# Two routing-weight matmuls folded into one, and short contractions padded to 128 rows, in a four-stage transformer kernel

## The reference

```python
x = x + tanh(g_xattn[0]) * L0_xattn(layernorm(x), ctx)
x = x + tanh(g_ffn[0])   * L0_ffn(layernorm(x))      # the mixture of experts
x = x + tanh(g_xattn[1]) * L1_xattn(layernorm(x), ctx, mask)
x = x + tanh(g_ffn[1])   * L1_ffn(layernorm(x))      # weights looked up in a table of 16
```

```python
# L0_ffn: 16 experts of width 64, the best 4 per token, and a shared expert of width 64
probs = softmax(h @ gate_w.T);  w, chosen = top_k(probs, 4);  w = w / w.sum()
comb[token, expert] = w where chosen, else 0
out = sum_e comb[:, e] * ((silu(h @ Wg[e]) * (h @ Wu[e])) @ Wd[e])
    + sigmoid(h @ shared_gate_w) * ((silu(h @ sWg) * (h @ sWu)) @ sWd)
# L1_ffn: width 688 = 5 * 128 + 48
out = (silu(h @ G.T) * (h @ U.T)) @ Dn.T
```

## Time and profile before

| | |
|---|---|
| median of three runs | 521.7 us |
| the profiled execution | 521.62 us, of which 519.8 us is the span from the first to the last instruction |
| TensorE | busy 436.0 us, 84% of the span |
| VectorE | 352.4 us, 68% |
| ScalarE | 199.7 us, 38% |
| GpSimd | 173.2 us, 33% |
| mean granted TensorE clock | 0.890 |

### The profile page before, as it was taken

One profiled execution on the slowest core, in us unless ns is written; L12 is line 12 of the kernel. 1 busy time (PEld: TensorE's weight loads), 2 busy tenths in 40 slices (PEclk: granted clock), 3 DMA queues, 4 the chain that ended last, 5 costly groups with the idle time before them and its releaser, 6 DMA issues.

```text
span 519.8 us, 9005 instructions
## 1 busy us (share of the span) xinstructions
PE 436.0 (84%) x3024; PEld 400.1 (77%) x3024; DVE 352.4 (68%) x769; ACT 199.7 (38%) x391; POOL 173.2 (33%) x207
## 2 busy tenths in 40 slices
PE   0465866958477999999998999989999998989996
PEld 0444856847367999999998988968987897788885
DVE  5767577584505668585855887798698879756642
ACT  2346445355220434343332443444354253423331
POOL 3104133231400221212134533653564355333332
PEclk9958785959657999999998969989987998999999
DMA  8111010100200020200101001001001000000000
GB/s 248 29 61 62 0 61 0 32 31 0 101 1 0 1 102 0 78 23 27 74 0 54 1 6 48 0 0 52 0 0 51 1 0 0 0 2 20 20 20 21
DMA packets 6629, 15.96 MB, mean 31 GB/s; under 512 B 1091, under 2 KB 4292, under 8 KB 6101
## 3 DMA queue, kind: packets, MB, share of 16 engines
q1 hardware_dynamic: 6612, 15.75, 9.2%
HBM read 14.70 MB, written 1.05 MB: 30 GB/s over the span
## 4 chain that ended last, share of the span: by engine, by line
PE 33%; issue 31%; POOL 15%; DVE 11%; ACT 6%; DMA 2%; POOLq 1%; DVEq 0%; ACTq 0%; SPq 0%
PE ps L289 19%; PE ps L484 5%; POOL workr L1010 4%; DVE work L1292 4%; PE ps L1086 3%; POOL work L1344 3%; POOL workr L1468 2%; PE ps L474 2%; POOL workA L565 2%; ACT workA L509 1%; POOL wB_lo L571 1%; POOL rstd L254 1%; PE ps L1098 1%; PE ps L359 1%; POOL wB_lo L1349 1%
## 5 line engine op out<-in xcount | busy, mean ns | idle before, releaser
L289 PE MATMUL ps<-xT_hi,wB_hi 128*128 128x256 f32 x224 | 65.7, 293 | 1.7 <-POOL wB_lo L1349 1.7
L289 PE MATMUL ps<-xT_lo,wB_hi 128*128 128x256 f32 x224 | 64.1, 286 | 0.0
L289 PE MATMUL ps<-xT_hi,wB_lo 128*128 128x256 f32 x224 | 63.9, 285 | 0.0
L289 PE MATMUL ps<-wB_hi,workr 128*128 128x256 f32 (+1 forms) x224 | 52.1, 296 | 4.5 <-POOL workr L1468 3.4
L289 PE MATMUL ps<-wN_hi,shared_r 128*128 128x256 f32 x256 | 52.8, 302 | 0.0
L1344 POOL TENSOR_SCALAR work<-work,lut_step,lut 128x344 f32<-128x344 int32 (+1 forms) x72 | 46.3, 659 | 1.7 <-POOL wB_lo L1349 1.6
L1010 POOL TENSOR_TENSOR workr<-work,workr 128x256 fp32r<-128x256 f32 (+1 forms) x36 | 22.9, 637 | 71.7 <-ACT workr L893 71.7
L1292 DVE COPY_PREDICATED work<-work 128x1376 f32<-128x1376 int32 (+5 forms) x36 | 43.6, 1212 | 4.0 <-DVE work L1292 1.1
L289 PEld LDWEIGHTS ps<-xT_hi,wB_hi 128*128 128x128 f32 x224 | 43.4, 194 | 2.4 <-issue 1.9
L289 PEld LDWEIGHTS ps<-wN_hi,shared_r 128*128 128x128 f32 x256 | 44.0, 206 | 1.5 <-DVE shared_r L1255 1.5
L289 PEld LDWEIGHTS ps<-wB_hi,workr 128*128 128x128 f32 (+1 forms) x224 | 38.4, 189 | 7.5 <-issue 6.2
(11 more groups left out here) (183 smaller groups left out, 1128.8 us busy)
## 6 DMA issues: line engine op xcount, KB each, us to landing
stage<-in_wC SPq DMA_DIRECT2D x4, 1280.0 KB, 5.5
stage<-in_wB SPq DMA_DIRECT2D x4, 768.0 KB, 4.3
stage<-in_idx SPq DMA_DIRECT2D x4, 536.0 KB, 4.0
stage<-in_wA SPq DMA_DIRECT2D x2, 512.0 KB, 5.4
out<-x SPq DMA_DIRECT2D x4, 256.0 KB, 2.2
x<-in_x SPq DMA_DIRECT2D x1, 768.0 KB, 6.7
ctx_T<-in_ctx_T SPq DMA_DIRECT2D x1, 512.0 KB, 7.1
ctx_n<-in_ctx_n SPq DMA_DIRECT2D x4, 128.0 KB, 2.1
```

The lines of the kernel that those rows point to most:

```text
L289: last = nc.tensor.matmul(out, l, r, start=start and i == 0, stop=stop and i == 2)
```

## The change

The two halves of the transposed routing weights go into one tile, `comb_rows`: the upper weights in rows 0 to 16, the lower ones in rows 32 to 48. `sel` has its table twice, in rows 0 to 16 and in rows 32 to 48. One matmul over 128 rows then gives the sum of both. In setup, one memset of GpSimd goes and ScalarE copies `sel` twice; the SyncE wait counts one more. The down products of the shared expert (before 64 rows) and of the last step of stage D (before 48 rows) run over all 128 rows. The added rows meet zeros: `sd` is padded with zero rows, and the padded gate columns of stage D are zero. In stage D the elementwise work of that step is now over 128 rows too; in stage B it stays at 64.

```diff
@@ constants, wS
+LOWER = 32
-            return (..., w[0:F, n:n + D],
+            return (..., w[:, n:n + D],
@@ act_A_start
-            act.wait_ge(padded, 3)
-            nc.scalar.copy(sel[0:E + 1]..., stage[0:E + 1, 0:NSEL]).then_inc(setup_act, 1)
+            act.wait_ge(padded, 2)
+            for r in (0, LOWER):
+                nc.scalar.copy(sel[r:r + E + 1]..., stage[0:E + 1, 0:NSEL]
+                               ).then_inc(setup_act, 1)
@@ tiles of stage B
-        combT_hi, combT_lo = (take_r(TG) for _ in range(2))
+        comb_rows = take_r(TG)
+        combT_hi, combT_lo = comb_rows[0:E + 1], comb_rows[LOWER:LOWER + E + 1]
@@ pe_B: spread(k)
-                nc.tensor.matmul(o, sel[:, k, :], combT_hi, start=True, stop=False)
-                nc.tensor.matmul(o, sel[:, k, :], combT_lo, start=False, stop=True).then_inc(*Bp["bc_done"].up())
+                nc.tensor.matmul(o, sel[:, k, :], comb_rows, start=True, stop=True).then_inc(*Bp["bc_done"].up())
@@ pe_B: down(k)
-                n = rows_B(k)
-                    last = mm3(ps[:, 6 + t, 0:D], h_hi[k % 3][0:n, t * P:(t + 1) * P],
-                               h_lo[k % 3][0:n, t * P:(t + 1) * P], d_hi, d_lo, k == 0, k == EC)
+                    last = mm3(ps[:, 6 + t, 0:D], h_hi[k % 3][:, t * P:(t + 1) * P],
+                               h_lo[k % 3][:, t * P:(t + 1) * P], d_hi, d_lo, k == 0, k == EC)
@@ stage D
         def rows_D(k):
-            return P if k < FC - 1 else FLAST
+            return P
@@ sync and tensor, setup
-            sp.wait_ge(setup_act, 2)
+            sp.wait_ge(setup_act, 3)
@@ gpsimd, setup
-            nc.gpsimd.memset(combT_hi.bitcast(F32), 0.0).then_inc(padded, 1)
-            nc.gpsimd.memset(combT_lo.bitcast(F32), 0.0).then_inc(padded, 1)
+            nc.gpsimd.memset(comb_rows.bitcast(F32), 0.0).then_inc(padded, 1)
```

More of the change, by code:

```diff
@@ L178, in wS @@
             n = DC * 2 * F
-            return (w[:, 0:n].rearrange("p (c n) -> p c n", c=DC), w[0:F, n:n + D],
+            return (w[:, 0:n].rearrange("p (c n) -> p c n", c=DC), w[:, n:n + D],
                     w[:, n + D:].rearrange("p (c n) -> p c n", c=DC))
@@ L630, in act_A_start @@
             act.wait_ge(sel_in, 16)
-            act.wait_ge(padded, 3)
-            nc.scalar.copy(sel[0:E + 1].rearrange("p k n -> p (k n)"), stage[0:E + 1, 0:NSEL]).then_inc(setup_act, 1)
+            act.wait_ge(padded, 2)
+            for r in (0, LOWER):
+                nc.scalar.copy(sel[r:r + E + 1].rearrange("p k n -> p (k n)"), stage[0:E + 1, 0:NSEL]
+                               ).then_inc(setup_act, 1)
         def act_A(act, g, more, two_more):
@@ L907, in act_B @@
             act.wait_ge(*Bp["combT_done"].at(g, 1))
-            nc.scalar.copy(combT_hi[0:E + 1], combT).then_inc(*Bp["combT_hi"].up())
+            nc.scalar.copy(combT_hi, combT).then_inc(*Bp["combT_hi"].up())
             upper(0)
@@ L983, in dve_B @@
             dve.wait_ge(*Bp["combT_hi"].at(g, 1))
-            nc.vector.tensor_tensor(combT_lo[0:E + 1], combT, combT_hi[0:E + 1].bitcast(F32),
+            nc.vector.tensor_tensor(combT_lo, combT, combT_hi.bitcast(F32),
                                     ALU.subtract).then_inc(*Bp["combT_lo"].up())
@@ L1522, in _ @@
             pe.wait_ge(setup_dve, 6)
-            pe.wait_ge(setup_act, 2)
+            pe.wait_ge(setup_act, 3)
             pe.wait_ge(*A["x_done"].at(GROUPS, 0))
```

## The result

| | Kernel before | Changed kernel |
|---|---|---|
| first comparison: median (lowest to highest of 14 runs) | 521.84 us (520.67 to 524.01) | 518.14 us (516.96 to 523.73) |
| ratio, 95% interval | | 0.994 (0.991 to 0.996) |
| a later comparison: median | 522.55 us (17 runs) | 520.14 us (12 runs) |
| ratio, 95% interval | | 0.995 (0.992 to 0.998) |
| profiled execution: time, span, clock | 521.62, 519.8 us, 0.890 | 521.0, 519.2 us, 0.887 |

The forecast was 517.6 us and faster; it came out at 518.1 and faster. The profiled execution of the changed kernel lay in the upper half of its runs. So the two spans must not be subtracted; what can be compared are periods of the same stretch at the same clock.

A forecast was written before the change was run, and what follows sets the result against it. TensorE was taken as the bound, with three waits per stage B group. Spread matmuls 3.84 plus D's row changes 0.27 gave 4.11 us off 521.62: 517.5, or 517.6 on the median; range 516.2 to 519.1.

The forecast's parts named there:

- The three points where TensorE waits: Stage B group: TensorE waits ahead of spread(0) 0.26 us, down(6) 0.35 and down(8) 0.31; gapless between.
- point 2: Stage B, ahead of down(6): TensorE waits 0.35 us for GpSimd's lower part, a chain starting at the end of gate_up(8).
- The spread matmuls: Stage B: 36 go at 0.12 us; spread(0) to spread(6) gain 0.84, spread(7) 0, spread(8) 0.12; 3.84 us over four groups.
- point 1: Stage B, ahead of spread(0): TensorE waits 0.26 us for VectorE's lower routing weights, timed by the end of the group before.
- 128 rows: Row change at group boundaries: 0.09 us each, 0.27 over three in D, 0 in B; entry free, added elementwise work 0.
- B's exits: Stage B, leaving the short product at group boundaries: gain 0, as VectorE is later at spread(0); other bound 0.27 us.
- Setup, 0: ScalarE's second sel copy, 1.15 us, taken as hidden in idle times: 0, bounded by 0 and 1.15.
- Halfway: Rival: slack at down(1) or VectorE mid-group runs out, half of 3.84 turns into waits; 519.7 us, chance 0.08.
- setup: Rival: the sel copy stands in the chain of waits and all of 1.15 us stays; 518.7 us, chance 0.05.
- nothing: Rival: the removed matmul was hidden, so the change does nothing; 521.6 us, chance 0.02.
- The rival with the row change at entries and B's exits: Rival: row change also costs at entry, 0.09 in 8 places, 0.72 us more, or B's exits count; 516.8 us, chance 0.04.
- The slower one: Rival: less dense TensorE work brings half-clock stretches in stage B, 1.5 us per group; 523.4 us, chance 0.03.

The follow-up runs named there:

- more3: Changed kernel with three further copies of spread(3)'s matmul in each group of B; groups of B 27.25, 27.24, 27.23 us.
- more7: Changed kernel with three further copies of spread(7)'s matmul in each group of B; groups of B 26.91, 26.88, 26.90 us.
- shift_only: Kernel before with two spread matmuls kept, but lower routing weights written to rows 32 to 48 and sel copied twice; ratio 1.0037 against the kernel before.
- aligned: Changed kernel with routing weights written twice side by side, so VectorE reads and writes rows 32 to 48 in place; ratio 0.9961 against the kernel before.
- twocopy: Changed kernel with halves exchanged: lower weights at rows 0 to 16, upper copied by ScalarE to rows 32 to 48; ratio 0.993 against the kernel before.
- setup6: Changed kernel with four more ScalarE copies of sel's size in setup, six in all; ratio 0.9993 against the kernel before.
- rows_only: Kernel before with only the 128-row edits; ratio 1.0001 against the kernel before.
- spread_only: Changed kernel without its 128-row edits (shared expert 64 rows, last step of D 48); ratio 0.9954 against the kernel before.

## Why the prediction was right, step by step

- **What bounds the kernel.** Right. The three points where TensorE waits held, and more3 and more7 showed the reading that the sum stood on: 0.12 us a matmul between points 1 and 2, nothing ahead of point 2.
- **The spread matmuls, 0.96 us a group.** Right: behind `spread(0)` every group gained 0.95, and more3 and more7 show which matmuls count. The count of 36 and the two waits came as forecast (0.47 ahead of `down(6)`; 0.33 for 0.31). The sum was short of a term, not the mechanism.
- **The term that was mis-sized: VectorE's lower weights.** The prediction took the duration of the nearest row, 0.40, and the duration did stay (0.41). The cost is in the starts: at rows 32 to 48, between neighbours that start at row 0, the instruction overlaps neither, 0.12 us ahead of it and 0.11 behind. The first stands on the path at point 1 in the three later groups: 3 x 0.12 = 0.4 us. So a group came to 26.90 and not to the 26.7 to 26.8 that was named as a sign of being right. Shown by shift_only (it alone, +0.12), aligned (not the shift) and twocopy (gone at rows 0 to 16); the rows of line 464, which the kernel before had, show that a change of start row goes with it. The prediction put nothing of it in the sum, and only asked what a doubled duration would cost.
- **128 rows.** The exit was priced at 0.09 and is 0.18, because the second matmul behind it is late too; I had read only the first distance. The elementwise work, "0 to 0.05 us per group, taken as 0", is 0.04 a boundary and 0.06 at the end. D gained 0.41 by its three periods and 0.35 in all, where 0.27 was forecast: the two errors partly cancel. B's exits gave nothing and the entry cost nothing (`down(8)` follows GpSimd by 0.15 us, before by 0.14), both as forecast; rows_only shows the first. The rule of the Trainium skill ("TensorEngine Tiling (Array Packing)", section Tiling Modes, Key Properties) that a change of mode drains TensorE agrees with the exit of stage D, at 0.18 us; at the entry, where a wait stands ahead, no run here shows a price.
- **Setup, 0.** Right: twocopy's profile shows the second copy free, and setup6 that 1.5 to 2.4 us of such work would be.
- **Sum.** 4.11 was forecast; the periods give 3.80 - 0.37 + 0.35 = 3.8, the medians 3.7 in the first comparison and 2.4 in the later one, each uncertain by more than 1 us. That the first median falls so near to the forecast is in part luck: the later one, 520.14, lies above the range of 516.2 to 519.1, as do single runs of the first. The periods are the better witness, and by them the forecast was 0.3 us too high.
- **Rivals.** Halfway is refuted by the 0.95 of 0.96 behind `spread(0)` (its 519.7 left the 0.27 of stage D out; with it, it would be 519.5), setup by twocopy and setup6, nothing by the ratio. The rival with the row change at entries and B's exits is refuted by rows_only. The slower one was a real mechanism that struck too seldom. But I gave the clock too small a place elsewhere: it moves single executions by more than the change's sum is uncertain, through stage A, which the change touches only in setup, and through the first group of B.
- **Still open.** Why an instruction of VectorE on other rows than its forerunner doesn't overlap it; whether it is the address of `h3` itself or its place relative to the two operands in `workr` that costs GpSimd 0.1 us, and whether other offsets do better; and what sets the clock in stage A. Whether 0.12 or less would remain with the lower weights moved off VectorE was not tried, nor whether the second copy can be left out of the first group's path.

## What to carry to other kernels

To price a matmul that goes or comes, take the distance between starts, and ask first whether the next wait of TensorE begins with an event behind it or beside it: here the same three matmuls a group cost 1.4 us or nothing. When an instruction moves to other partitions, its duration does not tell its cost: compare its start with its forerunner's, and the next one's with its own. When it moves to another address, even the duration can change. Look at the first round of a loop by itself: its waits can be others than those of the later rounds, as here, where the moved instruction cost nothing in the first round and the remedy cost 0.14 us. And when a kernel's runs scatter by more than the change is worth, count in periods of undisturbed stretches, each against the granted clock beside it.

## What the runs showed of the hardware

- VectorE: a subtraction of 17x256 took 0.40 to 0.41 us at either place, but started 0.60 after a 128x512 one at rows 0 to 16 and 0.71 to 0.72 at rows 32 to 48; its follower started 0.33 or 0.44 to 0.45 later. So it was in every undisturbed group, in ten profiles at rows 32 to 48 and in four at rows 0 to 16. In stage A, instructions over rows 32 to 63 overlapped a forerunner on the same rows by 0.07 us, and started 0.03 after the end of one on other rows.
- GpSimd: a subtraction of 128x256 took 0.64 us with the one input that lies in `work` 8 bytes past a multiple of 16, and 0.74 on a multiple of 16, counted from the start of `work`, in both stages and in both directions of the shift. The other input and the output stayed where they were. On the path this was worth 0.16 us in a group of D and 0.24 to 0.28 in one of B.
- TensorE: leaving a product of 48 rows for one of 128 cost 0.09 us at the first and 0.09 at the second matmul; leaving one of 64 rows for 18-column products, 0.09 and 0.02 (0.13 us to the second where 0.11 is usual there). After a wait the second matmul of 256 columns starts 0.19 to 0.20 us after the first, with 64 rows or 128; entering a 64-row product behind a wait cost nothing that shows.
- The clock: one stretch of 3.3 us at the 1.2 GHz level came in the midst of stage B in spread_only, at a group's start, and cost 0.94 us.
